# Local attention in a four-layer sequence kernel: keys projected and rotated first, the queries' norm applied while masking

## The reference

```python
def local_attention_layer(x, wqkv, qs, ksc, wo):          # x: 2 x 2048 x 256; 8 heads of 64
    q, k, v = jnp.split(shift_token(x) @ wqkv, 3, axis=-1)  # each 2048 x 512, then cut into heads
    q = l2norm(q) * qs                                      # t / max(norm(t), 1e-12), per head
    k = l2norm(k) * ksc
    q, k = rotary_xpos(q, k)          # x * cos * scale + rotate_half(x) * sin * scale (k: / scale)
    # windows of 128 queries, each against its own window's keys and the window before
    sim = jnp.einsum('bhwid,bhwjd->bhwij', 8.0 * windows(q), look_around(windows(k)))
    sim = jnp.where(mask, -huge, sim)                       # causal, no further back than 128
    out = jnp.einsum('bhwij,bhwjd->bhwid', softmax(sim), look_around(windows(v)))
    return x + merge_heads(out) @ wo
```

## Time and profile before

| what | value |
|---|---|
| median of 3 runs | 4441.09 us (4441.04 to 4442.19) |
| profiled execution: its own time / its span | 4444.75 us / 4443.1 us |
| instructions | 60919 |
| PE busy / weight loads | 3852.1 us (87%) / 1852.5 us (42%) |
| DVE busy | 2924.3 us (66%) |
| ACT busy | 2046.0 us (46%) |
| POOL busy | 894.0 us (20%) |
| mean granted clock of TensorE | 0.929 |

### The profile page before, as it was taken

One profiled execution on the slowest core, in us unless ns is written; L12 is line 12 of the kernel. 1 busy time (PEld: TensorE's weight loads), 2 busy tenths in 40 slices (PEclk: granted clock), 3 DMA queues, 4 the chain that ended last, 5 costly groups with the idle time before them and its releaser, 6 DMA issues. The chain is left out here.

```text
span 4443.1 us, 60919 instructions
## 1 busy us (share of the span) xinstructions
PE 3852.1 (87%) x20308; PEld 1852.5 (42%) x20308; DVE 2924.3 (66%) x6609; ACT 2046.0 (46%) x3685; POOL 894.0 (20%) x800
## 2 busy tenths in 40 slices
PE   7898977898978989898969899579899699888989
PEld 6233334233334545454533333343333355454545
DVE  3987766887756652665349787659787566436643
ACT  2365642365645541455124566324566455315541
POOL 1101013101023321332230010150010333223322
PEclk8799988799989999999988999888999899999999
DMA  3212002212010010000031110021110100100000
GB/s 79 40 18 40 3 2 48 32 16 41 4 58 8 1 48 6 21 6 6 19 68 30 30 30 1 2 50 30 30 30 1 60 6 1 49 25 6 1 10 24
DMA packets 127249, 108.94 MB, mean 25 GB/s; under 512 B 38568, under 2 KB 120016, under 8 KB 125904
## 3 DMA queue, kind: packets, MB, share of 16 engines
q1 hardware_dynamic: 126928, 104.92, 11.6%
HBM read 41.15 MB, written 4.19 MB: 10 GB/s over the span
## 5 line engine op out<-in xcount | busy, mean ns | idle before, releaser
L751 DVE TENSOR_REDUCE chunk_max<-banks 128x1 f32<-128x512 f32 (+3 forms) x2240 | 1396.2, 669 | 188.9 <-PE banks L645 123.0
L718 ACT ACTIVATE probs<-banks 128x1024 f32<-128x1024 f32 (+3 forms) x1280 | 1083.0, 895 | 833.5 <-PE banks L686 829.6
L642 PE MATMUL banks<-stack_k,stack_q 96*128 96x512 bf16 (+3 forms) x2560 | 846.8, 377 | 137.2 <-DMA stack_k<-parts 55.0
L686 PE MATMUL banks<-stack_q,stack_k 99*128 99x512 bf16 (+3 forms) x2560 | 662.5, 350 | 11.3 <-ACT probs L718 11.3
L663 PE MATMUL banks<-probs,values_group 128*17 128x512 f32 (+3 forms) x5120 | 594.6, 536 | 16.7 <-ACT probs L718 13.9
L642 PEld LDWEIGHTS banks<-stack_k,stack_q 96*128 96x128 bf16 x2560 | 251.0, 100 | 803.5 <-DVE chunk_max L751 524.4
L609 POOL TENSOR_SCALAR_AFFINE_SELECT probs<-probs 128x512 f32<-128x512 f32 x256 | 162.9, 636 | 1749.2 <-ACT probs L718 1746.6
L1311 ACT ACTIVATE probs_l<-probs_l,nmax 128x256 f32<-128x256 f32 x512 | 255.8, 500 | 455.8 <-DVE nmax L1428 455.8
L1208 PE MATMUL banks<-k_blocks,qT 128*128 128x512 f32 x512 | 293.4, 656 | 109.4 <-issue 104.0
L1188 PE MATMUL banks<-wqkv,hT 128*128 128x512 f32 x768 | 368.2, 618 | 2.4 <-issue 2.4
L1596 PE MATMUL banks<-hnT,w 128*128 128x512 f32 x768 | 342.0, 606 | 3.5 <-ACT hnT L1619 3.5
(11 more groups left out here) (183 smaller groups left out, 4767.4 us busy)
## 6 DMA issues: line engine op xcount, KB each, us to landing
stack_q<-parts SPq DMA_DIRECT2D x384, 64.0 KB, 2.4
stack_k<-parts SPq DMA_DIRECT2D x384, 64.0 KB, 2.4
xpos<-in_c_xpos SPq DMA_DIRECT2D x4, 2048.0 KB, 8.3
wqkv<-in_L_ffn_wqkv SPq DMA_DIRECT2D x12, 512.0 KB, 11.7
w<-in_L_ffn_w SPq DMA_DIRECT2D x16, 341.0 KB, 4.0
x_tok<-in_L_attn_x SPq DMA_DIRECT2D x8, 512.0 KB, 5.9
rope<-in_c_rope SPq DMA_DIRECT2D x2, 2048.0 KB, 7.7
hs_f<-x_mid SPq DMA_DIRECT2D x16, 256.0 KB
```

The source lines that it names most:

```text
L642: ins = pe.matmul(out, sq[0:KS, c, j0 + j, i * P:(i + 1) * P], sk[0:KS, cc, j0 + j, 0:width], start=True, stop=not diag, skip_group_check= ...
L686: ins = pe.matmul(ps[:, SCORE + j, off:CH], keys, sq[0:KS + PARTS, c, j, off:CH], start=True, stop=True, skip_group_check=True)
L718: act.activation(probs[:, s % 2, 2 * half:2 * half + 2, off:CH], ps[:, SCORE + 2 * half:SCORE + 2 * half + 2, off:CH], ACT.Exp)\
L751: dve.tensor_reduce(chunk_max[:, n % 2, j:j + heads, i, cc], bank[:, 0:heads * width].rearrange("p (h n) -> p h n", h=heads), AX.X, ALU.ma ...
```

## The change

- The keys are projected, squared, summed, clamped and rotated first; in DVE's order the keys' part now lies behind the scaling of pair 0, the queries' rotation around the scaling of pair 1, and the queries' squares behind the scaling of pair 2.
- `normalise` multiplies the keys alone, and it moves from pair 2 to pair 1. The queries are no longer multiplied by their inverse norm; the rotated sum in `prod_cos` is transposed as it is.
- The inverse norm of the queries becomes the `scale` operand of the masking instruction, one value per partition, where the constant 1.0 stood. It has two buffers, for even and odd windows.
- POOL's order per window becomes: power for the keys, addition for the keys, addition for the queries, power for the queries.
- In pair 3 PE transposes queries and keys ahead of the output product.

The diff, cut to its core:

```diff
-    PROJECTED = ((0, 1), (), (2,), ())
+    PROJECTED = ((1, 0), (), (2,), ())
...
+        inv_q, inv_k = sb("inv_norm_q", [P, 2, LH]), sb("inv_norm_k", [P, LH])
...
-                    for src, bank, ready, done in ((qn, BQ, "qn", "q_T"), (kn, BK, "kn", "k_T")):
+                    for src, bank, ready, done in ((pc[:, 0, :], BQ, "q_sum", "q_T"), (kn, BK, "kn", "k_T")):
...
                         if p == 3:
+                            if w + 1 < NT:
+                                turn_qk(w + 1)
                             if w:
                                 out(w - 1)
-                            if w + 1 < NT:
-                                turn_qk(w + 1)
...
-                    for i, rotated in enumerate(("rot_q", "rot_k")):
-                        own = slice(i * LH, (i + 1) * LH)
-
-                        pool.wait_ge(S["clamp"], 2 * w + i + 1)
-                        pool.tensor_tensor(inv_n[:, own], ssum[:, own], mhalf[:, own], ALU.pow).then_inc(S["inv_n"], 1)
-                        pool.wait_ge(S[rotated], w + 1)
-                        pool.tensor_tensor(pc[:, i, :], pc[:, i, :], psn[:, i, :], ALU.add).then_inc(S["sumsq"], 1)
+                    q, kk = slice(0, LH), slice(LH, 2 * LH)
+
+                    pool.wait_ge(S["clamp"], 2 * w + 1)
+                    pool.wait_ge(S["kn"], w)
+                    pool.tensor_tensor(inv_k[:, :], ssum[:, kk], mhalf[:, kk], ALU.pow).then_inc(S["inv_n"], 1)
+                    pool.wait_ge(S["rot_k"], w + 1)
+                    pool.tensor_tensor(pc[:, 1, :], pc[:, 1, :], psn[:, 1, :], ALU.add).then_inc(S["k_sum"], 1)
+                    pool.wait_ge(S["rot_q"], w + 1)
+                    pool.tensor_tensor(pc[:, 0, :], pc[:, 0, :], psn[:, 0, :], ALU.add).then_inc(S["q_sum"], 1)
+                    pool.wait_ge(S["clamp"], 2 * w + 2)
+                    if w >= 2:
+                        pool.wait_ge(S["maxed"], NP * (w - 1))
+                    pool.tensor_tensor(inv_q[:, w % 2, :], ssum[:, q], mhalf[:, q], ALU.pow).then_inc(S["inv_n"], 1)
...
                 def normalise(w):
                     dve.wait_ge(S["k_T"], w)
-                    for i, (dst, done) in enumerate(((qn, "qn"), (kn, "kn"))):
...
+                    dve.wait_ge(S["inv_n"], 2 * w + 1)
+                    dve.wait_ge(S["k_sum"], w + 1)
+                    r3 = inv_k[:, :].rearrange("p (h o) -> p h o", o=1).to_broadcast([P, LH, LD])
+                    dve.tensor_tensor(kn[:, :].rearrange("p (h d) -> p h d", h=LH),
+                                      pc[:, 1, :].rearrange("p (h d) -> p h d", h=LH), r3, ALU.mult).then_inc(S["kn"], 1)
...
-                                                       in1=m, scale=1.0, scalar=3e38, op0=ALU.add, op1=ALU.min,
+                                                       in1=m, scale=inv_q[:, w % 2, 2 * p + h:2 * p + h + 1], scalar=3e38, op0=ALU.add, op1=ALU.min,
...
-                    if p == 1 and ahead:
-                        squares(w + 1, 1)
                     maximum(n)
                     if p == 1 and ahead:
-                        rotate(w + 1, 1, (0,))
+                        rotate(w + 1, 0, (0,))
                     scale(n)
+                    if p == 0 and ahead:
+                        squares(w + 1, 1)
+                        rotate(w + 1, 1)
                     if p == 1 and ahead:
-                        rotate(w + 1, 1, (1,))
-                    if p == 0 and ahead:
+                        rotate(w + 1, 0, (1,))
+                        normalise(w + 1)
+                    if p == 2 and ahead:
                         squares(w + 1, 0)
-                        rotate(w + 1, 0)
-                    if p == 2 and ahead:
-                        normalise(w + 1)
```

More of the change, by code:

```diff
@@ L1132, in local_attention @@
     S = Stage(nc, k["pool"], "kept masks zero_x halves zero_k h_T h_T_out qk_q qk_k v_mm v_out "
-              "sq_q sq_k rot_q rot_k sumsq sum_q sum_k inv_n qn kn q_T k_T q_T_out k_T_out scored maxed exped rinv pn "
+              "sq_q sq_k rot_q rot_k q_sum k_sum sum_q sum_k inv_n kn q_T k_T q_T_out k_T_out scored maxed exped rinv pn "
               "p_T p_T_out pv o_T_out y x_out clamp")
@@ L1146, in local_attention @@
         sqr = sb("squares", [P, 2, INNER])
-        ssum, inv_n, mhalf = sb("ssum", [P, 2 * LH]), sb("inv_norm", [P, 2 * LH]), sb("mhalf", [P, 2 * LH])
-        qn, kn = sb("qn", [P, INNER]), sb("kn", [P, INNER])
+        ssum, mhalf = sb("ssum", [P, 2 * LH]), sb("mhalf", [P, 2 * LH])
+        inv_q, inv_k = sb("inv_norm_q", [P, 2, LH]), sb("inv_norm_k", [P, LH])
+        kn = sb("kn", [P, INNER])
         qT = sb("qT", [P, NP, P])
@@ L1247, in _ @@
                 turn_h(0)
-                for i, come in enumerate(("w_q", "w_k", "w_v")):
+                for i, come in ((1, "w_k"), (0, "w_q"), (2, "w_v")):
                     pe.wait_ge(early[come], 16)
@@ L1323, in _ @@
                 h_out(0)
+                square(0, 1)
                 square(0, 0)
-                square(0, 1)
                 v_take(0)
@@ L1398, in rotate @@
                     dve.wait_ge(S[squared], w + 1)
-                    dve.wait_ge(S["kn"], w)
+                    dve.wait_ge(S["kn" if i else "q_T"], w)
                     src = ps[:, bank, :].rearrange("p (h d) -> p h d", h=LH)
@@ L1413, in normalise @@
                     dve.wait_ge(S["k_T"], w)
-                    for i, (dst, done) in enumerate(((qn, "qn"), (kn, "kn"))):
[L1415 to L1420, removed]
+                    dve.wait_ge(S["inv_n"], 2 * w + 1)
[3 more added lines that the diff above has]
+                                      pc[:, 1, :].rearrange("p (h d) -> p h d", h=LH), r3, ALU.mult).then_inc(S["kn"], 1)
                 def maximum(n):
-                    w = n // NP
+                    w, p = n // NP, n % NP
+                    if p == 0:
+                        dve.wait_ge(S["inv_n"], 2 * (w + 1))
                     m = later[:, 0 if w == 0 else 1 if w % SLOT == 0 else 2, :]
@@ L1447, in add @@
                                       ALU.add).then_inc(S["x_out"], 1)
-                for i in range(2):
+                for i in (1, 0):
                     squares(0, i)
                 dve.wait_ge(early["tab_ready"], 4)
-                for i in range(2):
+                for i in (1, 0):
                     rotate(0, i)
```

## The result

The changed kernel takes 4473.32 us (median of 4, 4468.65 to 4478.96) against 4441.07: 1.0073 times as long, 95% interval 1.0056 to 1.0091. It is 32 us slower; 23 us faster was forecast, and the time lies outside the range. The profiled execution took 4472.1 us, 27 more than that of before.

What follows compares the result with a forecast made beforehand. Bound: a chain through DVE and ACT that ends PE's stall before each window's scores. Regular periods -20 us, stage starts -5, last windows +2: -23, giving 4418 us against 4441.09; 8-in-10 range 4392 to 4446.

Steps and rivals of the forecast that it cites:

- The chain: Dependent DVE and ACT work in each regular window: forecast to shorten from 18.44 to 18.11 us, 20 us over 60 periods.
- M1, M2, M3: DVE's maskings of pairs 1, 2, 3: forecast 6.84 us after the window's first scores, then 4.03 and 3.57 apart.
- next T0: Start of the next window's first scores on PE: forecast 3.66 us after pair 3's masking, factor's cost included.
- the factor: Per-partition scale in the masking instruction: forecast 57 ns a half, six halves on the chain, 0.34 us a period.
- a free factor: Rival 1: the masking's per-partition scale costs nothing, period 17.77 us, 45 us saved, 4396 us; chance 0.15.
- the clamp: DVE's clamp of the key sums in pair 0: held up by POOL to 1.10 us, forecast at 0.17 in all 64 places.
- the key multiplication: DVE's keys times inverse norm, after pair 1's scaling: forecast to start 0.16 us before POOL's query addition and keep 0.68.
- PE's stand: PE's wait before a window's first scores: 1.73 us before, forecast about 1.4 and counted as cover for later work.
- Rival 4: PE's clock: fewer or more long periods, a few us either way, +80 if in every period; chance 0.05 with anything else.
- Rival 3: POOL's query addition gets the port first and delays DVE's key multiplication 0.9 to 1.0 us a period: 4475 us; chance 0.12.
- the start of a stage: Query power moved behind both POOL additions: first scores up to 1.7 us earlier, 1.3 taken, 5 us over four stages.
- Turning ahead of the product: PE's transposes of queries and keys before the output product in pair 3: costed at nothing, the product still within PE's stall.

Runs made afterwards that it cites:

- e4: The changed kernel with the constant 1.0 as the masking's scale instead of the per-partition factor, leaving queries unnormalised; 4401.2 us.
- e8: e6 with the transposes of the next-but-one window's input, and ACT's copy of them, moved from pair 0 to pair 1; 4294.9 us.
- e5: The kernel before with two one-column copies on ACT ahead of the copy of qT in each window; 4506.9 us.
- e3: The changed kernel with a useless 512-column product on PE ahead of each window's first scores; 4418.5 us.
- e7: The changed kernel with a useless 128-column product on PE ahead of each window's first scores; 4417.6 us.
- e2: The kernel before with only PE's order in pair 3 changed: transposes of queries and keys ahead of the output product; 4437.6 us.
- e1: The changed kernel with only PE's order in pair 3 put back: output product ahead of the transposes; 4480.2 us.
- e6: The changed kernel with ACT's copies of the transposed queries and keys ahead of its exponentials of pair 3; 4330.1 us.

## Why the prediction was wrong

- **The chain was right, and a little short.** M1, M2, M3 and the next T0 came within 0.05 of their forecast, but each late: 18.22 for 18.11, so that 13 us were won and not 20. Of the 0.11, 0.02 is the factor; the rest is there without it (17.86 in e4, where a free factor was put at 17.77). The mechanisms were as forecast: the factor at 60 ns for 57, the clamp free at 0.17 in all its places (170 to 175 ns over 128), the key multiplication ahead of POOL and unhindered at 0.68.
- **The step that failed is PE's stand, taken as harmless cover.** I forecast "PE standing about 1.4 us", with PE's work carried over unchanged. PE's work shrank too, by 0.37, most likely since its operands lie ready earlier, so the stand grew to 1.89. (It follows that 1.7 us a period was not the most to be won: e8 won 2.15, 18.44 to 16.29.) And I priced the clock as "a few us either way", with one long period in every window as something "which nothing speaks for". It was 28 of 52, +42 us. Rival 4 named the clock, but for a shorter stand, and shared a chance of 0.05. e5 makes the same loss in the kernel before by lengthening the stand, e3 and e7 take it away by filling it.
- **The trace of before had the sign.** Its long periods were in the earlier trace rows with a clock of 0.91. Six of 52 at a stand of 1.73 was a sign that the stage stood close to where the clock falls; e2 (1.62, none) and e5 (1.92, 32) show how close. Any change to the stand had to be priced with the clock: +42 us, twice the gain that was forecast.
- **Rival 3 named nearly the time, 4475, for another reason; that is chance.** POOL did get ahead, but only at the start of a stage, where that multiplication lasts 1.67 (maximum of its line) and is off the path that mattered: from the stage's first transposes to its first scores it still takes 16.24 us for 17.88 in the first stage, and 5.5 us less in the four together, where 5 were forecast.
- **Turning ahead of the product, costed at nothing,** is worth nothing here (e1), and in the kernel before it moves and shortens the stand (e2). e6 moves the copies ahead of the exponentials with the transposes turned first; whether it needs them there was not run.

Open: in the regular periods the stand and PE's idle share of the period move together, so these runs alone don't tell which of them counts. The first periods of the stages speak for the single stand. Before, PE stands three times in window 0 of the first stage (1.67, 1.62 and 1.73 us), 5.0 of 20.9 us in all, and the clock, once up, doesn't fall; in e5 the last of the three is 1.92, and it falls behind it; in e4 the two stands are 0.64 and 2.84, 3.6 of 18.6 us, and it falls too. All four stages show the same. But the length of the stand doesn't settle a single period: at 1.89 about half of them are hit, and why those isn't shown.

## What to carry to other kernels

Where PE waits once in every period, write down how long it stands and how often the granted clock falls behind it, before and after the change; a shorter chain can leave PE standing longer when its own work shrinks as well. A few long periods in a regular loop are a warning, and the cheapest test is to lengthen or fill the stand and look at the clock. Then take the stand away rather than fill it: find the copy that ends it and see whether it waits only for its place in an engine's order.

## What the runs showed of the hardware

In this loop, with one stand in a period of 16 to 19 us, a stand of 1.89 us put TensorE at 1.2 GHz for a stretch in 28 of 52 periods, 1.92 in 32, 1.73 in 6, 1.62 and less in none; a long period of the kernel before and of the changed one takes 1.5 to 1.7 us more. A per-partition scale instead of a constant costs a masking instruction of 128x256 60 ns (421 to 481). Where a DVE multiplication of two SBUF tensors and a POOL addition met, the one that started 0.14 to 0.17 earlier kept its time (0.68 on DVE, 1.26 on POOL) and the other was stretched (to 1.65 and to 1.67). The rows of the second case, from the start of the changed kernel's first stage:

```profile
1328.73 1.26 POOL L1372 TENSOR_TENSOR prod_cos<-prod_cos,prod_sin 128x512 f32<-128x512 f32 x1
...
1328.87 1.67 DVE L1424 TENSOR_TENSOR kn<-prod_cos,inv_norm_k 128x512 f32<-128x512 f32 x1 [0.21 <-POOL prod_cos L1370]
```

The later one lost 0.38 and 0.99, a little less than the 0.51 and 1.12 for which the earlier one still ran. Not every pair meets so: before, POOL's power of 1.66 from 1329.34 left a DVE multiplication that started 0.18 behind it at 0.69.
